# Softmax layers of a four-layer model: row maxima reach the queries by DMA instead of through TensorE and VectorE

## The reference, cut to what matters

```python
# layer 0
scores = jnp.einsum('bhtd,bhsd->bhts', q, k)
attn_w = jax.nn.softmax(scores.astype(jnp.float32), axis=-1).astype(q.dtype)
...
# layer 1
scores = jnp.einsum('bthd,bshd->bhts', q, k) * scale
scores = jnp.where(key_mask, scores, -jnp.inf)
attn = jax.nn.softmax(scores, axis=-1)
out = jnp.einsum('bhts,bshd->bthd', attn, v).reshape(B, T, C)
```

## Time and profile before

| what | value |
|---|---|
| median of 3 runs | 2075.88 us (2075.8 to 2077.05) |
| the profiled execution | 2076.24 us, of which the span of the trace is 2074.4 us |
| TensorE busy | 1955.2 us, 94% |
| VectorE busy | 1574.4 us, 76% |
| ScalarE busy | 1386.3 us, 67% |
| GpSimd busy | 208.4 us, 10% |
| layer 0's reductions, L1069 | 512, 586.9 us busy |
| layer 1's reductions, L1069 | 256, 294.7 us busy |

### The profile page before, as it was taken

How to read it: one execution, slowest core, us unless ns; L and a number is a source line. 1 busy time by engine, 2 the same in 40 slices (tenths; PEclk the granted TensorE clock), 3 DMA queues, 4 the chain that set the end, 5 groups by cost and what they waited for, 6 DMA issues and landing times. The chain is left out here.

```text
span 2074.4 us, 43441 instructions
## 1 busy us (share of the span) xinstructions
PE 1955.2 (94%) x17202; PEld 858.4 (41%) x17202; DVE 1574.4 (76%) x2254; ACT 1386.3 (67%) x2761; POOL 208.4 (10%) x388
## 2 busy tenths in 40 slices
PE   8999999999999979999998999999999899999998
PEld 4222222222223422222233666666665344444453
DVE  7999999999995599999946667776774655555553
ACT  4899999999998549899875666666774422222253
POOL 3011111110111330111100000000000200000000
PEclk7999999999999979999999999999999999999999
DMA  3000010110101020101010011110111055555510
GB/s 102 2 24 20 23 31 16 31 25 14 32 11 28 1 57 12 30 19 41 8 29 6 13 26 26 26 26 16 23 23 39 14 128 121 122 122 120 120 45 21
DMA packets 76041, 82.63 MB, mean 40 GB/s; under 512 B 23744, under 2 KB 58560, under 8 KB 71888
## 3 DMA queue, kind: packets, MB, share of 16 engines
q1 hardware_dynamic: 74896, 79.06, 16.0%
q0 software_dynamic: 528, 0.43, 0.1%
q10 hardware_dynamic: 432, 0.56, 0.1%
HBM read 62.98 MB, written 2.42 MB: 32 GB/s over the span
## 5 line engine op out<-in xcount | busy, mean ns | idle before, releaser
L1069 DVE TENSOR_REDUCE a0nm<-ps 128x2 f32<-128x1024 f32 x512 | 586.9, 1215 | 11.0 <-PE ps L936 8.8
L1047 ACT ACTIVATE a0p<-ps 128x512 f32<-128x512 f32 x1024 | 544.1, 599 | 60.4 <-PE ps L956 43.6
L970 PE MATMUL ps<-a0p,a0vst 128*32 128x256 f32 x4096 | 328.0, 392 | 27.4 <-ACT a0p L1047 14.0
L1069 DVE TENSOR_REDUCE a1nm<-ps 128x2 f32<-128x1024 f32 x256 | 294.7, 1217 | 7.2 <-PE ps L936 6.3
L1047 ACT ACTIVATE a1p<-ps 128x512 f32<-128x512 f32 x512 | 275.6, 596 | 34.4 <-PE ps L956 25.5
L956 PE MATMUL ps<-a0qm,a0k 32*128 32x512 bf16 x1024 | 277.3, 387 | 0.0
L2157 ACT ACTIVATE ex_s<-ps 128x512 f32<-128x512 f32 x128 | 76.4, 597 | 253.0 <-PE ps L2112 253.0
L936 PE MATMUL ps<-a0k,a0q 32*128 32x512 bf16 x1024 | 203.5, 395 | 17.9 <-DVE a0nm L1069 15.7
L2246 DVE TENSOR_TENSOR ex_su<-ex_s,ps 128x512 f32<-128x512 f32 x128 | 88.0, 688 | 114.2 <-PE ps L2116 113.7
L1757 PE MATMUL ps<-cak,caq 64*128 64x512 f32 (+3 forms) x768 | 171.3, 521 | 2.1 <-DVE canm L1909 2.1
L970 PE MATMUL ps<-a1p,a1vst 128*32 128x256 f32 x2048 | 164.1, 393 | 6.4 <-ACT a1p L1047 5.5
(11 more groups left out here) (327 smaller groups left out, 2495.0 us busy)
## 6 DMA issues: line engine op xcount, KB each, us to landing
ex_wb<-ex_w_dram SPq DMA_DIRECT2D x62, 512.0 KB, 6.2
xc_res<-car_dram SPq DMA_DIRECT2D x32, 256.0 KB, 4.2
xc_res<-a0rec SPq DMA_DIRECT2D x15, 256.0 KB
a0q<-a0parts_sb SPq DMA_DIRECT2D x95, 32.0 KB, 2.0
a1q<-a1parts_sb SPq DMA_DIRECT2D x94, 32.0 KB
a0k<-a0parts_sb SPq DMA_DIRECT2D x90, 32.0 KB, 2.0
a1k<-a1parts_sb SPq DMA_DIRECT2D x84, 32.0 KB
f2wg<-in_ex_gate SPq DMA_DIRECT2D x32, 64.0 KB, 1.8
```

Source lines behind the costliest of these rows:

```text
L970: last = pe.matmul(R.ps[32 * j:32 * j + 32, 6, cols], vst[:, g, s, j * HG // 4, :], p[:, s % 2, j, cols], start=(g == 0 and s == 0 and hal ...
L1047: act.activation(p[:, s % 2, e, :], R.ps[:, score_bank(n), :], ACT.Exp).then_inc(exp_done, 1)
L1069: dve.tensor_reduce(nm[:, u % 2, tb, 2 - 2 * z:4 - 2 * z, hf], R.ps[:, bank:bank + 2, :], X_AXIS, ALU.max, negate=True).then_inc(bank_free, 1)
```

## The change

- No `turn` on TensorE, no `merge` and no `qm`. The scores read `q` itself, and the parts of the maxima are written into its spare rows.
- `split` has four operations on GpSimd. VectorE then transposes `mt` (128x64, bf16) in blocks of 32 into `mr` (the new `turn`), and SyncE issues eight DMAs a unit (`maxima_rows`) from `mr` to the spare rows. Each unit's first score waits until all eight have landed (`rows_in`).
- The queries of a group that is loaded later get one more DMA that puts zeros into the spare rows (`load_queries`).
- In layer 0 (`whole`) a maxima slot is one head with all 1024 keys, so `join` goes; its two products have the same rows of the array. In layer 1 `join` is a tensor_tensor of two operands.
- The maxima run 9 slots ahead, not 6 (`LEAD`). `turn(u + 1)` stands in step 4.

```diff
-    qm = sb("qm", [128, 2, RT, CW], BF16)
+    mt = sb("mt", [128, 4, 4, 4], BF16)
+    mr = sb("mr", [128, 2, 2, 32], BF16)
+    A.zero_rows = sb("zero_rows", [512 // ROWS, RT, T], BF16)
...
+def load_queries(A, idx, slot, queue):
+    load_rows(A, idx, slot, 0, queue)
+    if idx >= 4:
+        queue.dma_start(A.q[A.spare_rows, slot, :, :], A.zero_rows[:]).then_inc(A.ld[slot], 16)
...
-        slots = [(u + 1 + n // 16, n % 16) for n in (6 + 2 * s, 7 + 2 * s)]
+        slots = [(u + 1 + n // 16, n % 16) for n in (LEAD + 2 * s, LEAD + 1 + 2 * s)]
...
-        return s == 6 and u + 1 < UNITS
+        return s == 4 and u + 1 < UNITS
...
     def on_sp(sp):
...
+        def maxima_rows(u):
+            _k, chunk_i, _g, slot = place(u)
+            sp.wait_ge(mt_step, 2 * u + 2 if whole else 3 * u + 3)
+            for i in range(4):
+                for pair in range(2):
+                    rows = slice(7 + 64 * pair, 64 + 64 * pair, 8) if RT == 1 else A.spare_rows
+                    to = q[rows, slot, pair % RT, chunk_i * CW:chunk_i * CW + CW].rearrange("p (t i r) -> p t i r", t=4, i=4)
+                    sp.dma_start(to[:, :, i, :], mr[32 * i:32 * i + 32, u % 2, pair, :]).then_inc(rows_in, 16)
+        for u in range(3):
+            maxima_rows(u)
         for n in range(2 * PAIRS - 1):
...
             sp.dma_start(rec_dram[c].rearrange("r (a t) -> (r a) t", a=16), packed[:, c, :]).then_inc(rec_out[c], 16)
+            maxima_rows(2 * n + 3)
             sp.wait_ge(rec_out[c], times)
             sp.dma_start(rec[:, c, :], rec_dram[c].unsqueeze(1).broadcast_to([8, 16, CW])).then_inc(rec_in[c], 16)
             if c and kk < PAIRS:
                 sp.wait_ge(exp_done, (kk - 1) * 128)
                 load_group(A, 2 * kk, kk % 2 * 2, sp)
-                load_rows(A, 2 * kk + 1, kk % 2 * 2 + 1, 0, sp)
+                load_queries(A, 2 * kk + 1, kk % 2 * 2 + 1, sp)
...
+            if 2 * n + 4 < UNITS:
+                maxima_rows(2 * n + 4)
...
+            if whole:
+                rows, rt = rows_of(head_of(i))
+                for hf in range(2):
+                    pe.matmul(R.ps[:, bank + hf, :], q[rows, slot, rt, t0:t0 + 128],
+                              k[rows, slot, rt, hf * CW:(hf + 1) * CW], start=True, stop=True).then_inc(bank_full, 1)
+                return
...
         for u in range(UNITS):
-            pe.wait_ge(bank_free, emptied("turn", u))
+            pe.wait_ge(rows_in, 128 * (u + 1))
...
-            dve.tensor_reduce(m0[:], nm[:, u % 2], X_AXIS, ALU.min).then_inc(max_ready, 1)
+            dve.tensor_tensor(m0[:, u % 2], nm[:, u % 2, :, :, 0], nm[:, u % 2, :, :, 1], ALU.min).then_inc(mt_step, 1)
...
-            dve.tensor_tensor(qm[:, u % 2], q[:, slot, :, t0:t0 + CW], bf16_bank(dve_bank("turn", u)),
-                              ALU.add).then_inc(bank_free, 1)
+            dve.transpose(mr[:, u % 2].rearrange("p a r -> p (a r)"), mt[:].rearrange("p h k t -> p (h k t)")).then_inc(mt_step, 1)
...
-                if s == 5 and u < UNITS - 1:
-                    join(u + 1)
                 if slots[1]:
                     reduce(*slots[1])
+                if s == 3 and u + 1 < UNITS:
+                    join(u + 1)
                 if turns_at(u, s):
-                    merge(u + 1)
+                    turn(u + 1)
```

More of the change, by code:

```diff
@@ L159, in __init__ @@
         self.heads_of_group, self.mask = heads_of_group, mask
-        self.spare = (7, 15, 23)
+        self.spare_step = rows // 4
+        self.spare_rows = slice(7, 128, self.spare_step)
         self.scale = dim ** -0.5
@@ L166, in __init__ @@
         self.n_pool_loads = 4 * self.row_tiles
+        self.zero_rows = None
         self.inited = [nc.alloc_semaphore(name + "inited0"), nc.alloc_semaphore(name + "inited1")]
@@ L437, in load_mask @@
              .then_inc(A.ld[slot], 16)
+def load_queries(A, idx, slot, queue):
+    load_rows(A, idx, slot, 0, queue)
+    if idx >= 4:
+        queue.dma_start(A.q[A.spare_rows, slot, :, :], A.zero_rows[:]).then_inc(A.ld[slot], 16)
 def load_group(A, idx, slot, queue):
-    load_rows(A, idx, slot, 0, queue)
+    load_queries(A, idx, slot, queue)
     load_rows(A, idx, slot, 1, queue)
@@ L740, in softmax_stage @@
     PAIRS = NG // 2
+    LEAD = 9
     sb = lambda n, s, d=F32: ctx.enter_context(nc.sbuf_tensor(pre + n, s, d))
@@ L778, in slot_of, with head_of @@
         return i // 4, i // 2 % 2, i % 2
+    def head_of(i):
+        return (0, 2, 1, 3)[i % 4]
     def ahead(u, s):
-        slots = [(u + 1 + n // 16, n % 16) for n in (6 + 2 * s, 7 + 2 * s)]
+        slots = [(u + 1 + n // 16, n % 16) for n in (LEAD + 2 * s, LEAD + 1 + 2 * s)]
         return [x if x[0] < UNITS else None for x in slots]
     def turns_at(u, s):
-        return s == 6 and u + 1 < UNITS
[L789 to L794, removed]
+        return s == 4 and u + 1 < UNITS
+    turns = [("max", u, i) for u in range(UNITS) for i in range(16)]
     turns += [("spread",)]
@@ L865, in on_pool @@
         pool.memset(zero[:], 0.0).then_inc(pool_step, 1)
-        pool.wait_ge(pool_step, 3)
+        pool.memset(A.zero_rows[:], 0.0).then_inc(pool_step, 1)
+        pool.wait_ge(pool_step, 4)
         def stage_v(g):
@@ L928, in p1_slot @@
                 by_pool = 0 if slot else A.n_pool_loads
-                pe.wait_ge(ld[slot], 16 * ((kk // 2 + 1) * A.n_loads - by_pool))
+                pe.wait_ge(ld[slot], 16 * ((kk // 2 + 1) * A.n_loads + kk // 2 - by_pool))
                 if u == 0:
@@ L937, in p1_slot @@
                           k[rows, slot, rt, hf * CW:(hf + 1) * CW], start=True, stop=True).then_inc(bank_full, 1)
-        def turn(u):
-            pe.wait_ge(mt_ready, u + 1)
-            out = bf16_bank(wait_bank("turn", u))
-            for tb in range(4):
-                for r in range(RT):
-                    last = pe.transpose(out[:, r, tb * 128:(tb + 1) * 128],
-                                        mt[:].rearrange("p b h w -> p b (h w)")[:, tb, r * 128:(r + 1) * 128],
-                                        R.identb[:])
-            last.then_inc(bank_full, 2)
         def score(u, s, e):
@@ L956, in score @@
             pe.matmul(R.ps[:, score_bank(n), :], k[rows, place(u)[3], rt, s * 128:(s + 1) * 128],
-                      qm[rows, u % 2, rt, :], start=True, stop=True).then_inc(p2_full, 1)
+                      q[rows, place(u)[3], rt, place(u)[1] * CW:(place(u)[1] + 1) * CW], start=True, stop=True).then_inc(p2_full, 1)
         def pv(u, s, half):
@@ L987, in on_pe @@
                 A.among_maxima[i]()
-        for i in range(4):
-            p1_slot(1, i)
-        turn(0)
-        for i in range(4, 6):
+        for i in range(LEAD):
             p1_slot(1, i)
@@ L1012, in on_pe @@
                     pv(*before, 1)
-                if turns_at(u, s):
-                    turn(u + 1)
         def last_products():
@@ L1096, in on_dve @@
             reduce(0, i)
+        reduce(1, 0)
         join(0)
-        for i in range(4):
+        for i in range(1, 3):
             reduce(1, i)
-        merge(0)
-        for i in range(4, 6):
+        turn(0)
+        for i in range(3, LEAD):
             reduce(1, i)
```

48 lines of the change are left out of this document (25 added, 23 removed).

## The result

| | median | runs |
|---|---|---|
| before | 2076.47 us | 2075.8 to 2078.1, 4 runs |
| after | 2558.49 us | 2552.95 to 2561.21, 4 runs |

The ratio is 1.2317 (95% interval 1.2294 to 1.2339): 482 us slower, where 118 were forecast. The direction is right, the size is not, and the time lies far outside the range of 2130 to 2250.

What follows compares the result with a forecast made beforehand. VectorE was taken to set the pace, with TensorE and ScalarE close behind. To the profiled 2076.24 us it added 58 (layer 0), 40 (layer 1), 12 (starts) and 7 (clock), giving about 2194 us, range 2130 to 2250.

Steps and rivals of the forecast that it cites:

- the half step of layer 0: TensorE in layer 0: with two products on the same rows, 1.10 us instead of 0.88.
- the cover: Layer 0: TensorE's half step of 1.10 us just stays under VectorE's 1.133 us reduction.
- the sum: Terms added to the profiled time: 58 us in layer 0, 40 in layer 1, 12 for starts, 7 for the clock.
- The clock term: TensorE falls to its low clock in long waits, two half steps costing 0.9 us more each; 7 us taken.
- The lead: Layer 1: maxima nine slots ahead make keys due earlier; 3.1 and 0.75 us twice, 8 us.
- (c): Layer 0: TensorE becomes the bound through an exposed weight load, 1.22 us a half step, about 2230 us; chance 0.07.
- (b): SyncE's queue: new DMAs issue cheaply, 0.31 to 0.35 us each, about 2111 us; chance 0.08.
- (d): Both layers: maxima always land in time, only VectorE's relief counts, about 2060 us; chance 0.04.
- The queue: SyncE: maxima DMAs at 0.67 us each wait behind other DMAs, delaying units; 58 us in layer 0, 40 in layer 1.
- The starts: First scores of the layers come later, 4.6 us and 1 more in layer 0, 7.1 in layer 1; together 12.
- VectorE's relief: VectorE loses merge (0.59 us a unit), gains a 0.15 us transposition; units about 18.5 us in layer 0, 18.9 in layer 1.

Runs made afterwards that it cites:

- e3: Changed kernel with 28 extra full-array products ahead of layer 0's first score; 2503.49 us in one run.
- e11: Changed kernel with 28 extra products ahead of layer 0, LEAD 11, transposition in step 3, maxima DMAs issued by GpSimd; median 2083.76 us, two of seven runs near 2502.
- e9: Changed kernel with two heads a slot in layer 0, LEAD 10, transposition a step earlier, maxima DMAs issued by GpSimd; 2067.22 us.
- e7: Changed kernel with two heads a slot in layer 0 and LEAD 8 instead of 9, SyncE issuing the maxima DMAs; 2221.13 us.
- e1: Changed kernel with layer 0's maxima slots holding one key half of two heads again, all else kept; 2552.61 us.
- e2: Kernel before with one head a slot and no join in layer 0, lead 6, no maxima DMAs; 2704.32 us in one run.
- e4: e1 with GpSimd instead of SyncE issuing the maxima DMAs, right behind split; 2490.7 us.
- e5: Changed kernel with the 28 extra products of e3 and the maxima DMAs issued by GpSimd; 2492.94 us.
- e12: e11 without the 28 extra products; 2492.66 us.
- e6: Kernel before with the maxima seven slots ahead instead of six, nothing else changed; 2232.93 us in one run.
- e10: e9 with SyncE instead of GpSimd issuing the maxima DMAs; 2222.22 us.

## Why the prediction was wrong, step by step

**The step that failed** is the half step of layer 0: "I take this for layer 0 after the change: it is under VectorE's 1.133, so the cover just holds." The figure itself was right: 1.10 is what e3 and e11 show with shared rows at a clock of 1.00, and there the cover nearly holds (a unit of e11 lasts 18.62 us, one of e9 18.45). Left out was the other level. The rows on which 1.10 rested, of layer 1, were all taken at 1.00; with three row groups at 0.50 the half step is 1.98, and the kernel stays there. Nor was layer 1 a fair stand-in: its heads take 64 rows each, so the four products of its half step still cover all 128 rows, and in after its clock came back behind a wait of 25.1 us (0.69 from 1200 to 1210 us, 1.00 in the next ten). Layer 0 grew by 389 us where the sum had 58; these 331 are most of the 364 by which the forecast was off. Most of the 18 us between the layers goes with it, since the last unit of layer 0 runs at the low level too: from the last transposition to the last `pv` it is 39.4 us, where the kernel before has 20.2 from its last merge. A few us of that are only the transposition's earlier place; e9, which has it still earlier and the high level, needs 26.9.

**The clock term** assumed the reverse: "Between nothing and 14 us: I take 7", because it would fall for two half steps after a long wait and come back. That is how e7 behaves, with four row groups. With three or two it does not come back by itself in after, e1, e2, e3, e4, e5 and e12; in e6 it did once, late, with a turn. A row could have warned: from 40 to 50 us of the kernel before, TensorE was busy for 6.99 us at 0.50, more than the "half the time" that I gave it. The Trainium skill (TensorE: Matmul & The Clock Gate, Part 1 on the clock gate) says that activity releases the throttle and that the low level belongs to an idle TensorE. By the busy share the trace of after does not agree: TensorE was busy for 99.34 of 100 us at 0.50. What the chip itself counts as activity is in no trace here. With four row groups (e7) the runs agree with it.

**The lead.** I costed `LEAD` 9 only for what comes due earlier. Its odd parity puts both heads of a neighbouring score between scores 0 and 1. That by itself is enough: e6 (157 us) and e1 against e7 (331 us) show it. In the change the one head a slot makes three groups out of it, which is no better, and with one head a slot no lead can give more than three.

**The rivals.** (c) was the nearest: TensorE the bound of layer 0, through rows used twice. Its mechanism was another, an exposed weight load at full clock, its 1.22 a half step stands in none of the timelines read, and its 2230 was far off. (b) and (d) are out: the issue is not cheap (0.583 us).

**The queue**, which carried the forecast's sum, was right, and so was the direction that it gave; e7 and e10 show it with most of the clock's trouble taken away. The first eight maxima DMAs of after, and the first score:

```profile
56.30 5.15 SPq L850 DMA_DIRECT2D a0q<-a0mr  x8
...
62.64 0.58 PE L975 MATMUL ps<-a0q,a0k 32*128 32x512 bf16 x1 [0.74 <-DMA a0q<-a0mr]
```

They keep SyncE for 5.15 us (5.4 forecast) and the score starts 6.34 after the first (6.4). Layer 0 in e10 takes 699.5 - 49.9 = 649.6 us; the forecast's 586.1 + 58 is 644. Layer 1 takes 353.6, of which 23 are the wait at its start; 330.5 stay, and 290.1 + 40 is 330.

**The starts** were mis-sized. In layer 0 the first score was forecast at 56.8 and came at 62.64, since with one head a slot the maxima ahead of it came slower: with the slots of e1 it comes at 56.3. In layer 1 7.1 was forecast; in after TensorE waits 25.1 for the rows, and its first score comes 130.1 us behind the last `pv` of layer 0 (1200.6 - 1070.5) where it was 101.8 before (759.5 - 657.7), so 28.3 later. I took SyncE to be free at 760.2, from a row that a stretch had cut off at that end. The whole queue of the kernel before there reads:

```profile
756.21 7.78 SPq L430 DMA_DIRECT2D a1k<-a1parts_sb  x12
764.04 1.26 SPq L436 DMA_DIRECT2D a1k<-pj1mrow  x2
765.34 7.50 SPq L430 DMA_DIRECT2D a1q<-a1parts_sb  x12
772.88 8.31 SPq L430 DMA_DIRECT2D a1k<-a1parts_sb  x12
781.23 1.25 SPq L436 DMA_DIRECT2D a1k<-pj1mrow  x2
```

SyncE is busy up to 782.5, and the maxima of the first unit would wait behind that. With 25 for 7 the forecast's sum is 2212, with 28 it is 2215, and e7 and e10 measured 2221 and 2222. So for a kernel with the same queue and four row groups, the working would have been right within 10 us; with the lead and pairing as they are, it left out the largest effect. One slip in it is small: 40 DMAs of 0.68 us are 27.2, not 27.0.

**VectorE's relief** was right too: 18.5 and 18.9 us a unit forecast, 18.45 and 18.71 in e9. The transposition takes 0.235 us, not 0.15, and the reduction of one head's 1024 columns is no dearer than that of two of 512 (1.208 us in e11, 1.211 in e9).

**What stays open.** Why the chip leaves TensorE at 0.50 while its queue is full is not shown; the runs show only which orders do it. How many different row groups it takes was not varied finely: with 4 it rose in every traced run; with 3 and 2 it did so only with products or transposes over all 128 rows just ahead. Whether the number of groups decides, or how closely the products follow each other, which changes with it (1.55 or 1.98 us a half step at 0.50), no run tells apart. Four groups are no promise either: one untraced run of the kernel before, in the last group, took 2987.48 us at a mean clock of 0.615, where its others there have 0.979 to 0.982. Nor is it known why only one of e6's turns tipped it, why one wait in e3 lost the clock and an equal one did not, and why two of seven runs of e11 took 2502 us.

## What to carry to other kernels

Where products use only part of the array's rows, count the different row groups in each round of the loop, before and after a change of order, and price the round at both clock levels: a cover of 3% read at 1.00 is none if the loop can settle at 0.50. An index shifted by one can do that, so look at parity whenever a lead changes. For small DMAs on a shared queue, add up everything that is issued ahead of them from rows that are not cut by the window, and ask which engine's queue is free: moving these from SyncE to GpSimd was worth 155 us with four row groups (e10 to e9).

## What was not expected of the hardware

- A TensorE that is busy for 99 to 100 us of 100 can keep a granted clock of 0.50 for 975 us (after), through a whole stage, when its 32-row products share rows.
- The same loop holds either level: 2084 or 2502 us for one program (e11). The high one was lost behind a wait of 1.23 us (e5) and one of 1.97 us (e3), but not behind one of 1.98 us (e3, earlier); products over all 128 rows brought it (e3, e11).
- With four row groups the clock came back after every wait in layer 0, up to 6.5 us long: no window of 20 us in e7's layer 0 lies wholly at 0.50.
- GpSimd takes a median of 0.541 us to issue one of the maxima's DMAs (e9), SyncE 0.583 (after). I had priced only SyncE's.
